# Turning the next group's context ahead of a group's last product, in the preparation of a four-layer perceiver decoder

## The reference, cut to what matters

```python
# layer 0, one head of 256
scores = (xn @ W_q) @ (ctx @ W_k).T / 16          # 128 x 12544
# layers 1 and 3, 16 heads of 16
k = ctx @ Wk.T + bk          # 12544 x 256
v = ctx @ Wv.T + bv
# layer 3 alone: keys masked by mask_BxS2
# layer 2, 16 heads of 64
v = ctx @ Wv                 # 12544 x 1024
```

## Time and profile before

| What | Value |
|---|---|
| Median of 3 runs | 2990.39 us (2987.64 to 2991.67) |
| The profiled execution's own time | 2986.41 us |
| Its span in the trace | 2984.7 us |
| Preparation in the trace | from 3.65 us to about 752 us |
| TensorE busy over the span | 93% |
| Mean granted TensorE clock | 0.965 |

### The profile page before, as it was taken

The page is one execution under the profiler, slowest core; times in us unless marked ns, Lnnn a source line. Parts: engine busy times, 40 slices in busy tenths (PEclk is TensorE's granted clock), DMA queues, the critical chain, the costliest instruction groups (busy, mean ns, idle before and its releaser), DMA issues. The chain is left out here.

```text
span 2984.7 us, 66864 instructions
## 1 busy us (share of the span) xinstructions
PE 2786.4 (93%) x24069; PEld 1862.3 (62%) x24069; DVE 1769.0 (59%) x3578; ACT 1500.5 (50%) x2407; POOL 718.7 (24%) x389
## 2 busy tenths in 40 slices
PE   7999999999898799999989999999999788999988
PEld 5555555555668466666556666666665685666678
DVE  3232323323143677887748888888888617888532
ACT  2333333333341488888336666666666333666521
POOL 2423232232000000000006666666666000000000
PEclk9999999999999799999999999999999698999989
DMA  6887877877725999997622222222222375655455
GB/s 210 290 268 255 252 255 256 252 256 240 251 98 183 405 390 390 390 392 279 225 101 67 66 67 65 66 66 64 67 64 66 99 233 128 169 158 155 120 210 182
DMA packets 331565, 578.28 MB, mean 194 GB/s; under 512 B 79792, under 2 KB 265976, under 8 KB 325752
## 3 DMA queue, kind: packets, MB, share of 16 engines
q1 hardware_dynamic: 331408, 576.06, 57.7%
HBM read 394.96 MB, written 181.04 MB: 193 GB/s over the span
## 5 line engine op out<-in xcount | busy, mean ns | idle before, releaser
L1762 POOL TENSOR_TENSOR l2x_sums<-l2x_sums,all_S 128x768 f32<-128x768 f32 (+1 forms) x195 | 474.6, 2434 | 189.4 <-ACT all_S L2086 183.6
L1966 DVE TENSOR_TENSOR all_S<-all_S,l2x_minus 128x1024 f32<-128x1024 f32 x224 | 381.9, 1705 | 1.9 <-ACT l2x_minus L2082 1.9
L1803 PE MATMUL l2x_key_bank<-ahead_ctx,early_nat_out 128*64 128x512 f32 (+1 forms) x1536 | 323.1, 541 | 0.0
L652 PE MATMUL prep_work<-prep_wv,prep_ctxT 128*128 128x512 f32 x688 | 300.3, 594 | 0.0
L1947 DVE TENSOR_TENSOR l2x_tops<-l2x_scores,l2x_tops 128x768 f32<-128x768 f32 (+1 forms) x208 | 223.4, 1074 | 117.6 <-PE l2x_scores L1819 117.6
L1399 ACT ACTIVATE l3x_pT<-l3x_turned 128x896 f32<-128x896 f32 x224 | 197.5, 916 | 145.4 <-PE l3x_turned L1249 140.5
L2086 ACT ACTIVATE all_S<-all_S 128x1024 f32<-128x1024 f32 x224 | 213.3, 952 | 96.9 <-DVE all_S L1966 96.9
L1148 ACT ACTIVATE all_S<-all_S,l1x_negmax 128x896 f32<-128x896 f32 x224 | 233.0, 1044 | 44.8 <-DVE l1x_negmax L1084 25.6
L991 PE MATMUL l1x_turned<-all_ident,all_S 128*128 128x128 f32 x1568 | 221.3, 282 | 21.7 <-ACT l1x_pT L1059 13.7
L1834 PE MATMUL l2x_out<-all_S,l2x_values 128*64 128x128 f32 x3136 | 226.3, 285 | 11.1 <-ACT all_S L2086 11.1
L2074 ACT COPY all_S<-l2x_scores 128x1024 f32<-128x1024 f32 x224 | 201.8, 901 | 65.4 <-PE l2x_out L1834 63.7
(11 more groups left out here) (685 smaller groups left out, 4694.1 us busy)
## 6 DMA issues: line engine op xcount, KB each, us to landing
l1x_bias<-in_fside_Bx16xSxS_dram SPq DMA_DIRECT2D x112, 896.0 KB, 7.2
scratch_k<-prep_kparts SPq DMA_DIRECT2D x84, 672.0 KB, 3.3
l1x_k_half<-scratch_k SPq DMA_DIRECT2D x32, 1568.0 KB, 9.8
l2x_values<-scratch_v SPq DMA_DIRECT2D x112, 256.0 KB, 2.6
scratch_k<-prep_kparts SPq DMA_DIRECT2D x56, 448.0 KB, 5.1
scratch_v<-prep_st_v SPq DMA_DIRECT2D x11, 2048.0 KB, 9.2
scratch_v<-prep_st_v SPq DMA_DIRECT2D x14, 1536.0 KB, 7.2
l2x_values<-scratch_v SPq DMA_DIRECT2D x112, 192.0 KB, 2.3
```

What stands on the lines that cost most here:

```text
L652: last = nc.tensor.matmul(w[:, h, :], ctxT[:, k, j * P:(j + 1) * P], wv2[:, k, h * 512:(h + 1) * 512], start=(k == 0), stop=(k == KT - 1))
L1762: nc.gpsimd.tensor_tensor(sums[odd][:, 0:n], sums[odd][:, 0:n], in_memory(u), ALU.add).then_inc(added, 1)
L1803: last = nc.tensor.matmul(keys_ps[u % 2][half * VW:(half + 1) * VW, 0:n], wk_cur[odd][:, k, :], ahead.piece[u // 2][:, k, c:c + n], start= ...
L1966: nc.vector.tensor_tensor(part, part, minus[:, :].unsqueeze(1).to_broadcast([P, blocks_of(u), P]), ALU.add).then_inc(shifted, 1)
```

## The change

TensorE's part that turns a group becomes a function of its own, `turn_group`. It is called once ahead of all groups for group 0, and then, in each group but the last, for the next group just ahead of the group's last product. `s0` no longer waits for all copies at once: its first half waits for turns 0 and 1, its second half for turns 2 and 3. `take_turned` for the next group is called in VectorE's and ScalarE's programs at the same place, ahead of the copy of the last product. Every turn's copy now waits for the products: the turn that holds the block of the last product (turn 3 in a long plan, block 6; turn 1 in a short plan, block 2) for all of them, the others for all but the last.

```diff
@@ -488,6 +488,10 @@
                 one(g, plan)
             one(GRP - 1, plan)
 
+        def is_last(g):
+
+            return isinstance(g, int) and g == GRP - 1
+
         def rank(i):
 
             return sum(p[2] == plan[i][2] for p in plan[:i + 1])
@@ -611,7 +615,7 @@
                 last.then_inc(qfT_in_psum, 1)
                 pe.wait_ge(qfT_ready, 1)
                 pe.wait_ge(wide_loaded, 16)
-                def group(g, plan):
+                def turn_group(g):
                     pe.wait_ge(ctx_loaded, g * 16 + 16)
                     for t in range(TURNS):
 
@@ -621,10 +625,11 @@
                                                        ctx_nat[:, c, k * P:(k + 1) * P], com.ident[:, :])
                         last.then_inc(turn_in_psum, 1)
 
-                    for e in "vs":
-                        pe.wait_ge(turn_copied[e], g * 2 + 4)
+                def group(g, plan):
                     for i, (what, j, _e) in enumerate(plan):
                         w = work[:, i % 2]
+                        if i == len(plan) - 1 and not is_last(g):
+                            turn_group(g + 1)
 
                         if i >= 2:
                             e, before = plan[i - 2][2], done(plan[i - 2][2], g) + rank(i - 2)
@@ -642,6 +647,10 @@
                         pe.wait_ge(freed[e], before)
                         if what in ("s0", "k1", "k3"):
                             for h in range(2):
+                                if what == "s0":
+
+                                    for e in "vs":
+                                        pe.wait_ge(turn_copied[e], g * 2 + 3 + h)
                                 for k in range(KT):
                                     lhs = qfT[:, k, :] if what == "s0" else wT[what][:, k, j * P:(j + 1) * P]
                                     last = nc.tensor.matmul(w[:, h, 0:HB], lhs, ctxT[:, k, h * HB:(h + 1) * HB],
@@ -659,16 +668,20 @@
                                                             ctxT[:, k, c * P:(c + 1) * P], wT[what][:, k, :],
                                                             start=(k == 0), stop=(k == KT - 1))
                         last.then_inc(work_full, 1)
+                turn_group(0)
                 each_group(pe, group)
 
-            def take_turned(eng, copy, g, ts):
+            def take_turned(eng, copy, g, ts, plan):
+                last_block = plan[-1][1]
 
                 for t in ts:
                     eng.wait_ge(turn_in_psum, g * TURNS + t + 2)
                     if t == ts[0]:
 
                         eng.wait_ge(ctxT_stored, g * 16 + 16)
-                        eng.wait_ge(work_full, filled(g))
+                    if not (isinstance(g, int) and g == 0):
+
+                        eng.wait_ge(work_full, filled(g) - (0 if last_block // 2 == t else 1))
                     n = 2 if t < 3 else 1
                     copy(ctxT[:, :, 2 * t * P:(2 * t + n) * P].rearrange("p k (c q) -> p c k q", q=P),
                          turn[:, t, 0:n * 2 * P].rearrange("p (c k q) -> p c k q", k=KT, q=P)
@@ -717,8 +730,6 @@
                 dve.wait_ge(ones_set, 4)
                 dve.wait_ge(bias_loaded, 16 * 2 * (P // HEADS))
                 def group(g, plan):
-                    take_turned(dve, nc.vector.tensor_copy, g, (0, 2))
-
                     dve.wait_ge(mask_loaded, g * 16 + 16)
                     nc.vector.tensor_copy(mask[:, :], mask_u8[:, :]).then_inc(mask_ready, 1)
                     dve.wait_ge(mask_ready, g + 2)
@@ -729,6 +740,8 @@
                     for i, (what, j, e) in enumerate(plan):
                         if e != "v":
                             continue
+                        if i == len(plan) - 1 and not is_last(g):
+                            take_turned(dve, nc.vector.tensor_copy, g + 1, (0, 2), plan)
                         if what in ("v1", "v2", "v3"):
                             take_values(dve, nc.vector.tensor_copy, g, what, j, i).then_inc(freed["v"], 1)
                             for step in steps_at("v", g, i):
@@ -754,6 +767,7 @@
                         nk += 1
                         if isinstance(g, int) and g == LATE - 1 and i == FRONT_AT["v"]:
                             states.vector_front(dve)
+                take_turned(dve, nc.vector.tensor_copy, 0, (0, 2), plan)
                 each_group(dve, group)
                 states.vector_end(dve)
 
@@ -762,9 +776,10 @@
                 norm_scalar(act)
                 act.wait_ge(qfT_ready, 1)
                 def group(g, plan):
-                    take_turned(act, nc.scalar.copy, g, (1, 3))
                     nk = 0
                     for i, (what, j, e) in enumerate(plan):
+                        if i == len(plan) - 1 and not is_last(g):
+                            take_turned(act, nc.scalar.copy, g + 1, (1, 3), plan)
                         if e == "s":
                             take_values(act, nc.scalar.copy, g, what, j, i).then_inc(freed["s"], 1)
                             if isinstance(g, int) and g == LATE - 1 and i == FRONT_AT["s"]:
@@ -783,6 +798,7 @@
                             act.wait_ge(rest_ready, g * 4 + nk + 1)
                             nc.scalar.copy(parts[:, 1, :], kf[nk % 2][:, :]).then_inc(mid_ready, 1)
                             nk += 1
+                take_turned(act, nc.scalar.copy, 0, (1, 3), plan)
                 each_group(act, group)
 
             @block.gpsimd
```

## The result

The changed kernel takes 2976.4 us (median of 6 runs, 2972.1 to 2979.8) against 2989.8 us for the kernel before (6 runs): a ratio of 0.9957, with a 95% interval of 0.9946 to 0.9967. That is 13.4 us by the medians and 12.9 us (9.9 to 16.1) by the ratio. Forecast were 11.5 us, 2978.9.

What follows compares the result with a forecast made beforehand. TensorE, busy for 93% of the span, was taken as the bound. Ten long boundaries at 1.15 us and zero for the three short ones gave 11.5 us, from the 2990.4 median to 2978.9 us; range 2974 to 2986.

Steps and rivals of the forecast that it cites:

- The gain of a long boundary: At each of ten boundaries into long groups, TensorE's empty time before s0 goes: 1.15 us each, 11.5 us in all.
- the copies lay inside product 15: Before a long boundary, VectorE's 1.28 us and ScalarE's 0.59 us of turn copies fit under product 15's 3.43 us.
- turn 3 came inside the first half of `s0`: At long boundaries, turn 3 is copied 0.65 us after product 15, within s0's first half of 1.5 us; cost zero.
- VectorE was ready: Behind the last product, VectorE finishes copy, mask and fill 0.7 us before s0's result needs it.
- `s0` waiting at its start: Without a split wait, s0 would stand for turn 3 at a long boundary: 0.65 us each.
- The hole in the DMA queue: Empty DMA time before a long group's key parts shrinks from 3.2 to 0.45 us, stays open, and the gain is kept.
- the rival on the slower side: In groups 4 to 13, key parts queue behind the late wide store: 2.6 us a group slower, 3016 us; chance 0.06.
- the break-even: In long groups, the slower rival decides when the 11.5 us full DMA run grows by over 1.6 us.
- Short boundaries: At three boundaries between or out of short groups, turn 1 waits about 0.9 us; gain taken as zero, 0.75 either way.
- the best case given: For the three short boundaries together, the most that could be gained: 0.75 us.
- ScalarE's DMA wait: In groups 1, 2 and 3, waits of 1.91, 1.32 and 2.51 us take up the short boundaries' 0.25 us gain.
- The branch of the loop: Directly ahead of s0, an exposed 108 ns branch would cost 1.0 us over nine returns, leaving 10.5 instead of 11.5.

Runs made afterwards that it cites:

- the first two runs: Kernel before with only s0's wait split in halves: 2983.2 us; changed kernel with s0 waiting for all four turns before its first half: 2989.2 us.

## Why the prediction was right

*The gain of a long boundary* was put at 1.15 us and is 1.14 (54.87 less 53.73), within 0.02 us at eight boundaries, and 1.06 at the last one. Its working held in each step: the transposes took 1.52 us for 1.53 to 1.6, the copies lay inside product 15, turn 3 came inside the first half of `s0`, and VectorE was ready 0.64 us early for 0.7. That `s0` waiting at its start would cost 0.65 was a little low, 0.78.

*The hole in the DMA queue* was to shrink from 3.2 to 0.45 us and is 0.6. That the gain depends on this hole staying open was shown by filling it: 2.3 us of transfer more per group cost the kernel before nothing and the changed kernel its gain, and 3.2 us turned it into a loss, of 0.8 to 1.1 us a group through the queue and of 2.6 and more where TensorE's clock fell as well. So the consequence that the rival on the slower side warned of lay close, though its own way to it, a late wide store that alone overfills the queue, did not come. I had put the break-even at 1.6 us more; it lies at about 2.3. Of the 1.7 us by which that overran the hole, 1.5 came out at ScalarE and 1.1 in the period. The fall of the clock stood in no term of mine.

*Short boundaries* were put at zero and brought 0.23, 0.10 and, with group 3's own long boundary taken off (1.19 less 1.14), 0.31 and 0.05: 0.7 us, close to the best case given, 0.75. The step that failed was that ScalarE's DMA wait would absorb it. The waits there were 2.03, 1.25 and 2.54 us for 1.91, 1.32 and 2.51: the landing moved with the group. Single periods scatter here (41.28 and 41.84 for the second, 54.48 and 53.85 for group 3's, in the two profiles of the changed kernel); the sum of the four is 177.86 and 177.79.

*Left out:* the split also serves group 0, which has no boundary. Its `s0` waited 0.84 to 1.54 us in seven profiles with the split and 2.19 in an eighth, and 1.87 to 2.84 in four without. The split's 0.68 us would make the sum 12.0 + 0.7 = 12.7, and the ratio says 12.9, with an interval of 9.9 to 16.1 that can't tell the two sums apart. For group 0 this is argued from the long boundaries and not shown: the two sets of waits overlap.

*The branch of the loop.* By the Trainium skill's page Advanced Engine Details and Errata, section Control Flow Timing, which gives 108 ns for a compare-and-branch, an exposed one would, by an estimate from that page, have left 1.15 - 0.11 = 1.04 us a boundary. The measured 1.14 gives no sign of it.

## What to carry to other kernels

A wait on a whole tile can be split where the consumer reads it in parts; this gave 60% of the gain of a long boundary with an edit of a few lines. Moving the producer earlier brought 0.36 us by itself and 0.46 on top of the split. Before moving work ahead on an engine that is nearly full, look at what the same step postpones in the DMA queue: the step draws on the idle stretch ahead of the next transfer that someone waits for, and how much of it is left can be measured by adding a transfer there. A wait on TensorE can cost more than its length: where the clock fell behind it, the next product took some 1.6 us longer. When a wait names an engine's copy, look at what stands in front of that copy in the engine's queue: it decides which one of several alike is worth moving.

## What was not expected of the hardware

In the profile of the kernel before, TensorE's granted clock fell at the first `s0`, after the engine had stood still for 1.87 us:

```profile
23.30:27.00 3.70, 3.70 (x6) 1.76 (x7) 1.13 (x2) 0.00 (x0) 0.00 (x0) 0.55 0.57 144
```

0.55 of full speed is close to the lower level, 1.2 GHz, and that `s0` took 4.97 us for 3.27. In the profiles with the additional transfers in the kernel before, where this code is the same and TensorE had stood still for 2.48 and 2.41 us, it ran at 1.00 and took 3.27. So these 1.7 us belong to one execution, not to the kernel; I had first counted them to the change, and the expectations of the first two runs carry that error.

The length of the wait does not tell whether the clock falls. With 896 KB more in the kernel before, the same product `v3` 4, at full clock up to its wait both times, ran once at 1.00 and once not, in groups 1 and 3:

```profile
91.78 2.86 PE L659 MATMUL prep_work<-prep_T_v,prep_ctxT 128*128 128x256 f32 x12 [2.30 <-ACT prep_st_v L695]
...
178.65 4.54 PE L659 MATMUL prep_work<-prep_T_v,prep_ctxT 128*128 128x256 f32 x12 [2.28 <-ACT prep_st_v L695]
```

In the nine long periods with 1344 KB in the changed kernel it fell after 2.07 us and stayed after 2.25. What decides it is not shown.
